# Cross attention on one core: the division of the weighed values moves from the end of even steps to the end of odd ones, one step behind the turning of the bank

## The reference

```
w = softmax(scores + mask)
attn_output = w @ v
a_scores = tanh(gate) * softmax(q @ a_k^T * inv_sqrt_d)      # keys and values of the context
attn_output = attn_output + a_scores @ a_v
return attn_output @ Wo                                      # the heads side by side
```

## Time and profile before

| | |
|---|---|
| median of three runs | 2858.89 us (2856.67 to 2861.43) |
| the profiled execution | 2858.66 us |
| its span | 2856.9 us |
| PE busy | 2723.1 us (95%) |
| weight loads busy | 1688.1 us (59%) |
| DVE busy | 1829.7 us (64%) |
| ACT busy | 1315.4 us (46%) |
| GpSimd busy | 548.5 us (19%) |
| granted clock of PE, mean | 0.982 |

### The profile page before, as it was taken

One profiled execution on the slowest core, in us unless ns is written; L12 is line 12 of the kernel. 1 busy time (PEld: TensorE's weight loads), 2 busy tenths in 40 slices (PEclk: granted clock), 3 DMA queues, 4 the chain that ended last, 5 costly groups with the idle time before them and its releaser, 6 DMA issues. The chain is left out here.

```text
span 2856.9 us, 80959 instructions
## 1 busy us (share of the span) xinstructions
PE 2723.1 (95%) x34198; PEld 1688.1 (59%) x34198; DVE 1829.7 (64%) x5116; ACT 1315.4 (46%) x3201; POOL 548.5 (19%) x690
## 2 busy tenths in 40 slices
PE   6999999999999999999999889999999999986998
PEld 3565655656555565555656556666666666653466
DVE  5565555556556555565656537888888988886533
ACT  3343343434334343343434226666766676774131
POOL 1222212122221222222122132132131221200020
PEclk9999999999999999999999889999999999998999
DMA  5010110110101101101101100000000000001341
GB/s 186 23 36 12 31 46 20 31 29 20 43 17 32 35 13 31 35 13 31 46 2 32 61 31 1 13 7 7 13 1 13 13 2 13 2 1 62 144 185 67
DMA packets 96777, 99.97 MB, mean 35 GB/s; under 512 B 38177, under 2 KB 84385, under 8 KB 95265
## 3 DMA queue, kind: packets, MB, share of 16 engines
q1 hardware_dynamic: 96256, 94.27, 10.3%
q0 software_dynamic: 160, 0.52, 0.0%
HBM read 89.93 MB, written 4.85 MB: 33 GB/s over the span
## 5 line engine op out<-in xcount | busy, mean ns | idle before, releaser
L202 PE MATMUL dr_p<-x_t,dr_w_g 128*128 128x512 f32 x1536 | 742.0, 610 | 11.0 <-DMA dr_w_g<-in_w_in 7.6
L1259 ACT ACTIVATE xa_probs<-xa_probs,xa_low 128x256 f32<-128x256 f32 x1024 | 430.2, 497 | 18.2 <-DVE xa_low L1426 13.8
L202 PEld LDWEIGHTS dr_p<-x_t,dr_w_g 128*128 128x128 f32 x1536 | 268.9, 191 | 227.8 <-issue 217.6
L1191 PEld LDWEIGHTS xa_t<-ident,xa_probs 128*128 128x128 f32 x2048 | 224.6, 141 | 159.3 <-ACT xa_probs L1259 97.8
L1191 PE MATMUL xa_t<-ident,xa_probs 128*128 128x128 f32 x2048 | 286.0, 280 | 21.8 <-ACT xa_probs_t L1265 15.3
L636 DVE SCALAR_TENSOR_TENSOR dr_acc<-dr_p,dr_taps,dr_acc 128x510 f32<-128x510 f32 (+2 forms) x384 | 285.2, 743 | 23.4 <-ACT dr_acc L494 15.5
L1426 DVE CUSTOM_DVE_ANT_0 xa_probs<-xa_s,xa_mask 128x256 f32<-128x256 f32 x512 | 209.6, 409 | 77.5 <-PE xa_s L1178 77.5
L1265 ACT ACTIVATE xa_probs_t<-xa_t 128x512 f32<-128x512 f32 x256 | 152.5, 596 | 230.2 <-PE xa_t L1191 230.2
L1426 DVE CUSTOM_DVE_ANT_0 xa_probs<-xa_s,xa_zeros 128x256 f32<-128x256 f32 x512 | 214.6, 419 | 0.0
L1435 DVE COPY xa_probs_t<-xa_t 128x512 f32<-128x512 f32 x256 | 176.4, 689 | 41.6 <-PE xa_t L1191 30.4
L854 POOL TENSOR_TENSOR dr_first<-dr_n_mat,dr_packed 32x256 f32<-32x256 f32 x128 | 92.1, 719 | 505.1 <-DVE dr_n_mat L762 499.5
(11 more groups left out here) (308 smaller groups left out, 4741.3 us busy)
## 6 DMA issues: line engine op xcount, KB each, us to landing
dr_alpha<-alpha_rows SPq DMA_DIRECT2D x64, 254.0 KB
dr_w_g<-in_w_in SPq DMA_DIRECT2D x48, 256.0 KB, 6.0
dr_alpha<-alpha_rows SPq DMA_DIRECT2D x32, 256.0 KB
ff_wide<-in_fw_qkv SPq DMA_DIRECT2D x8, 1024.0 KB, 15.3
x_t<-in_x_t SPq DMA_DIRECT2D x4, 1024.0 KB, 7.3
tokens<-in_x_tok SPq DMA_DIRECT2D x1, 4096.0 KB, 15.7
dr_wo_g<-in_w_out SPq DMA_DIRECT2D x8, 512.0 KB, 3.7
xa_ctx_b<-in_ctx_t SPq DMA_DIRECT2D x8, 512.0 KB, 3.9
```

The costliest lines, as they stand in the source:

```text
L202: mm = pe.matmul(bank[:, :], w_g[:, k, m, :], x_t[:, k, 2 * S * batch:2 * S * (batch + 1)], start=(k == 0), stop=(k == KC - 1))
L1191: mm = pe.transpose(bank_t[i % 2][:, at:at + P], probs[:, v % 3, i, kind, kt * P:(kt + 1) * P], ident)
L1259: op = act.activation(at, at, ACT.Exp, bias=low[:, v % 3, i, kind:kind + 1], scale=-1.0)
```

## The change

The call of `share` in an even step u, for group u // 2 - 1, is gone. It stands at the end of an odd step instead: step u = 3 does group 0, step 5 group 1 and so on, each group one step later than before and in the same place in its step, behind the taking of an output tile and ahead of `turn_back` and `rate`. Step 127 does none. Group 62, which would be its own, is done behind the loop, after the last but one `choose` and before the turning of group 63. The instructions themselves, their number and their semaphores are the same.

```diff
@@ -1457,13 +1457,14 @@
                     tops(u + 1, 2, 3)
                 if ended(u, 1):
                     dve_take(dve, ended(u, 1))
-                if u and u % 2 == 0:
+                if u > 1 and u % 2 and u + 1 < LAST:
                     share(dve, u // 2 - 1)
                 if u % HALVES in BACK and u // HALVES + 1 < B:
                     turn_back(dve, BACK[u % HALVES], u // HALVES + 1)
                 if u % HALVES == 9 and u > HALVES:
                     rate(dve, u // HALVES - 1)
             choose(dve, B - 2)
+            share(dve, LAST // 2 - 2)
             turn_mixed(dve, LAST // 2 - 1)
             share(dve, LAST // 2 - 1)
             for use in TAIL:
```

## The result

The median of four runs is 2898.75 us (2897.09 to 2901.47), against 2860.16 us for four runs of the kernel before (2856.67 to 2861.55). The ratio is 1.0144, with a 95% interval of 1.0129 to 1.0158: slower by 1.4% (the two medians alone give 1.0135). The forecast was 2908 us in a range of 2887 to 2922. What follows is read from one profiled execution of each kernel, 2858.66 us before and 2901.47 us after; they lie 42.8 us apart, the medians 38.6 us.

A forecast was written before the change was run, and what follows sets the result against it. The prediction took PE (the tensor engine) to bound the cross attention stage. It summed 2858.7 us, 35.7 us of delays and 13.6 us of clock falls to 2908.0 us, range 2887 to 2922 us.

The forecast's parts named there:

- PE bounds the stage, and the vector engine counts only by its lateness: Cross attention, 128 steps: vector engine work counts only where it makes PE late, costing 4.4 us in 760 us before.
- Nothing is freed in even steps: Ends of even steps: taking the block away frees 0.04 us, taken as zero.
- Place 0: Step number modulo 16 is 0: block ahead of `choose` costs its full 1.59 us in six batches, 9.5 us.
- Place 8: Block at the end of place 7 costs 1.55 us in six batches, 1.3 us in batch 7; 10.6 us.
- its 0.21 us over the pace: Place 8 before the change: 6.54 us long where 6.33 us is the pace, cited beside the vector engine's chain without waits.
- Place 10: Block before `rate` at place 9: 0.56 us spare, 1.03 us lost in six batches, 1.6 us in batch 7; 7.8 us.
- Places 12 and 14: Block at place 11 meets GpSimd's second product, 0.72 us, 5.0 us in all; at place 13 0.2 us passes on, 1.4 us.
- The end: Behind the loop: last but one group's block costs 1.59 us less some 0.2 us step 127 gains, 1.4 us.
- The clock: PE's clock falls after longer gaps: five at place 0, half of six at place 8; 8 x 1.7 = 13.6 us.
- The price of one fall: PE's stretch at about half clock: a fall of 3.4 us loses half of it, 1.7 us.
- The rival without falls: Whole kernel: all the delays but no fall of PE's clock, 2894.4 us, range 2887 to 2898; chance 0.24.
- The rule of the Trainium skill: PE's clock: only idle gaps longer than any added here matter, so it stays and the 13.6 us term drops out.

The follow-up runs named there:

- `choose` elsewhere: Kernel after, with `choose` moved from the head of place 0 to the end of place 4; 2885.46 us, ratio 1.0106 to the kernel before.
- the last kernel: Kernel before, with `choose` at the end of place 3, second queries turned back at place 8, count taken ahead of the bank's turning there; 2849.53 us, ratio 0.9981.
- the kernel with the filled wait: Kernel after, with eight projection passes put into PE's wait at place 0 in batches 2 to 6; ratio 1.0148 to the kernel before.
- only place 15: Kernel before, with only the divisions of groups turned at place 14 moved, to the end of place 15 (group 62 behind the loop); ratio 1.0064.
- keys first: Kernel after, with the first keys taken ahead of the turning of the bank at place 10; ratio 1.0141 to the kernel before.
- only place 7: Kernel before, with only the divisions of groups turned at place 6 moved, to the end of place 7; ratio 1.0036.

## Why the prediction was right, and where it was not

- *PE bounds the stage, and the vector engine counts only by its lateness.* Right. PE's waits for the first copy grew from 3.5 to 28.8 us, to 25 waits, 25.3 us more of the 31.4 us by which the steps of batches 0 to 6 are longer without falls. Waits for the taking of the first keys add 3.0 us; the row of the second copy is unchanged at 0.9 us, and the last 3 us are in no wait that the profile lists.
- *Nothing is freed in even steps.* Right: no even step got shorter, and moving four groups of eight was worth nothing in either direction (1.0004, 0.9994 to 1.0014).
- *Place 0.* Right: 1.52 to 1.56 us against 1.59. It showed only because `choose` stands behind it, as the kernel with `choose` elsewhere proves (7.44 us).
- *Place 8.* Right in size, 1.53 against 1.55 us; batch 7 was taken 0.5 us too low. My remark that its 0.21 us over the pace came from the vector engine's chain was wrong: with the second queries turned back elsewhere it stayed at 6.54 us. The shared bank makes 0.12 us of it, as the last kernel showed; the other 0.09 us stay open.
- *Place 10.* Mechanism right, size wrong. The step that failed is that 0.56 us are spare between the second copy and the weighing, so that only 1.03 us are lost. I looked at the copies only. Between them stands the taking of the first keys, for which the second projection waits with no slack, because all pieces go through one bank (the wait of 0.50 us, gone when the keys are taken first). The chain up to that point had nothing to spare, so the block cost 1.56 and not 1.03 us, 3.6 us in all.
- *Places 12 and 14.* The meeting with GpSimd came as worked out, 0.69 against 0.72 us, and the long pairs of L1353 stand where the forecast had them: seven in the blocks at the end of place 11, seven at the end of place 5, no others. The 0.2 us at place 14 were a guess on the high side (0.07).
- *The end.* 2.5 us behind the stage, less the 0.17 us that step 127 gained, instead of 1.4. The wait of PE grew from 5.65 us to 7.20 us, by the block's length; the rest is clock, as the output projection behind it took 6.42 instead of 5.43 us.
- *The clock.* Forecast 8 falls, 13.6 us; measured 4 at place 0, none at place 8, and fewer in batch 7: 4.1 us. This is the mis-sized term that put the forecast 6.5 us above the profiled execution (2901.47 us); it covers 9.5 us, and place 10 gives 3.6 us the other way. The two errors partly cancel, and that is luck: with place 10 right the forecast would have been 2911.6 us. The price of one fall (1.7) was right within 0.1 us. The rival without falls had its mechanism wrong, as the stretches at the lower level show, but its 2894.4 us lie nearer to the median of 2898.75 us than the forecast does (4.4 against 9.3 us), because the clock cost 4.1 us in all and not 13.6.
- *A wait left out.* The sum of the clock took no account of batch 7, where the wait at place 0 grew from 1.81 us to 3.38 us; the falls there still cost 2.4 us less than before. In the kernel with the filled wait batch 7 has the same wait at place 0 (3.37 us) without this gain, so the wait does not bring it. Where it comes from stays open; without it the clock would have cost 6.5 us.

The rule of the Trainium skill that I weighed ("TensorE: Matmul & The Clock Gate", section "Why this matters for your kernels") would have had no falls at places 0 and 8 of batches 2 to 6. The measurement decides: there are falls after waits of 1.42 and 2.17 us, in 16 of 45 cases of this study, and none in five with PE kept busy in the wait of place 0.

## What to carry to other kernels

Before a block moves, follow the chain of its engine from its new place to the next thing that the bounding engine waits for, and count every hand-over on the way, a taken bank too, not only the copies that the profile shows as waits today. If the chain has no pause, the block costs its full length, however idle the engine is on average; a pause takes off what it is long (1.17 us ahead of the minima of place 14 left 0.07 us of 1.59). A wait for another engine that the block meets at its new place, as for GpSimd ahead of place 12, is part of its length. Even load is no aim in itself: put long pieces ahead of steps in which the bounding engine has other work between its waits, and keep them apart from each other.

## What the runs showed of the hardware

Whether a wait of TensorE of 1.4 to 2.2 us brings a fall of its clock is not fixed by its length. In one profiled execution of each kernel, in batches 2 to 6, waits of 2.17 us at place 0 brought a fall in 4 of 5 cases (kernel after), 4 of 5 (only place 15) and 1 of 5 (keys first). The wait of 1.42 us at place 8, in batches 1 to 6, brought 0 of 6 (kernel after), 2 of 6 (only place 7), 0 of 6 (filler), 4 of 6 (keys first) and 1 of 6 (`choose` elsewhere). In each of these falls the lower level lasts 3.4 us and costs 1.2 to 1.7 us. What decides between two equal waits stays open; a forecast can only count a share of them, and within one kernel the cases need not be independent of each other.
